# A two-layer block on one Trainium2 core: one projection in every attention slot, and the work between stages and the first x laid out anew

## The reference, cut to what matters

```python
ffn_out = x + gelu(x @ w1 + b1) @ w2 + b2
xq = x + (q_out @ pu_w + pu_b) * abs(q_scale)
out = where(vol > 0.5, xq, ffn_out);  x = layernorm(out) * ln_g + ln_b
```

```python
x = _ln(src) * (1.0 + scale) + shift
scores = q @ k.T / sqrt(32) + attention_bias;  scores = where(src_mask, -inf, scores)
ctx = softmax(scores) @ v
x = x + (ctx @ Wo + bo);  h = _ln(x) * g2 + beta2
return x + _gelu2(h @ W1 + b1) @ W2 + b2
```

## Time and profile before

| | |
|---|---|
| time, median of 3 runs | 2408.28 us (2406.91 to 2420.22) |
| profiled execution | 2410.64 us, its span 2408.8 us, clock granted 0.997 |
| TensorE busy | 98% of the span |
| VectorE, ScalarE, GpSimd busy | 56%, 42%, 42% |
| attention, first slot to the first matmul of L1 | 799.09 to 1685.44 us |

### The profile page before, as it was taken

The page is one execution under the profiler, slowest core; times in us unless marked ns, Lnnn a source line. Parts: engine busy times, 40 slices in busy tenths (PEclk is TensorE's granted clock), DMA queues, the critical chain, the costliest instruction groups (busy, mean ns, idle before and its releaser), DMA issues. The chain is left out here.

```text
span 2408.8 us, 42244 instructions
## 1 busy us (share of the span) xinstructions
PE 2368.5 (98%) x16104; PEld 1896.9 (79%) x16104; DVE 1355.8 (56%) x2749; ACT 1010.2 (42%) x2057; POOL 1018.5 (42%) x829
## 2 busy tenths in 40 slices
PE   9999999999999899999999999998999999999999
PEld 7788888888887677777777777776888888888887
DVE  7354454454457777777777777778443333323332
ACT  6132232231332776767666676767311211111111
POOL 0042241431424896767676776767112112202200
PEclk9999999999999999999999999999999999999999
DMA  7110111101123466565656565574420110110100
GB/s 230 45 44 18 44 35 44 44 17 61 44 80 111 148 192 199 158 209 162 201 163 198 168 200 184 173 209 156 131 71 1 52 52 0 52 52 0 52 35 18
DMA packets 142197, 243.94 MB, mean 101 GB/s; under 512 B 14140, under 2 KB 28620, under 8 KB 142048
## 3 DMA queue, kind: packets, MB, share of 16 engines
q1 hardware_dynamic: 140992, 241.40, 31.3%
q10 hardware_dynamic: 1056, 0.52, 0.1%
HBM read 216.69 MB, written 25.20 MB: 100 GB/s over the span
## 5 line engine op out<-in xcount | busy, mean ns | idle before, releaser
L1251 POOL TENSOR_TENSOR at_bias<-at_bias,at_mask 128x512 f32<-128x512 f32 x512 | 592.7, 1186 | 239.2 <-DMA at_bias<-in_fside_Bx16xSxS 226.7
L647 ACT ACTIVATE L_hid<-bank,L_b1c 128x512 f32<-128x512 f32 x256 | 176.6, 690 | 961.6 <-PE bank L290 961.4
L843 DVE CAST L_hh<-L_hid 128x512 fp32r<-128x512 f32 x256 | 121.7, 475 | 743.2 <-PE bank L970 714.5
L288 PE MATMUL bank<-xth,L_w1h 128*128 128x512 f32 x1024 | 402.7, 393 | 0.5 <-DVE L_w1l L714 0.5
L289 PE MATMUL bank<-xth,L_w1l 128*128 128x512 f32 x1024 | 399.5, 390 | 0.0
L290 PE MATMUL bank<-xtl,L_w1h 128*128 128x512 f32 x1024 | 399.4, 390 | 0.0
L968 PE MATMUL bank<-L_w2h,L_hh 128*128 128x512 f32 x1016 | 398.0, 392 | 0.0
L970 PE MATMUL bank<-L_w2l,L_hh 128*128 128x512 f32 x1016 | 395.6, 389 | 0.0
L969 PE MATMUL bank<-L_w2h,L_hl 128*128 128x512 f32 x1016 | 395.4, 389 | 0.0
L1307 ACT ACTIVATE at_bias<-at_bias,cos_sin 128x512 f32<-128x512 f32 x512 | 363.2, 713 | 3.9 <-DVE cos_sin L1448 3.5
L1448 DVE CUSTOM_DVE_ANT_0 at_bias<-bank,at_bias 128x512 f32<-128x512 f32 x512 | 331.6, 683 | 35.0 <-PE bank L1638 23.5
(11 more groups left out here) (213 smaller groups left out, 3242.2 us busy)
## 6 DMA issues: line engine op xcount, KB each, us to landing
at_bias<-in_fside_Bx16xSxS SPq DMA_DIRECT2D x256, 512.0 KB, 3.6
L_ring<-in_L_cond_w SPq DMA_DIRECT2D x32, 256.0 KB, 5.0
L_xres<-in_x SPq DMA_DIRECT2D x8, 1024.0 KB, 5.3
x_scratch<-L_xres SPq DMA_DIRECT2D x8, 1024.0 KB, 4.3
at_xres<-x_scratch SPq DMA_DIRECT2D x32, 256.0 KB, 4.4
L_xin<-x_scratch SPq DMA_DIRECT2D x8, 1024.0 KB, 5.6
L_xres<-x_scratch SPq DMA_DIRECT2D x8, 1024.0 KB, 5.5
L_xin<-in_x SPq DMA_DIRECT2D x7, 1024.0 KB, 5.1
```

Source lines behind the costliest of these rows:

```text
L288: nc_mm = pe.matmul(out, ah, bh, start=i == 0, stop=False)
L647: nc.scalar.activation(hid[m % 2][:, :], turn[m % 2][:, :], func, bias=b1c[:, m:m + 1]).then_inc(h_act, 1)
L1251: nc.gpsimd.tensor_tensor(tile, tile, mask[:, m % TT, :], ALU.add).then_inc(masked, 1)
```

## The change

Four things are moved; nothing is added to or taken from the arithmetic, except that two of the matmuls on zeros at the start go.

1. The slots of attention. The outputs stand in slots 0, 1, 2 and 3, one each; q and k in 4 to 7, 10, 11, 14 and 15 (batch 0 keeps one more in slot 0, where there is no output yet); v in 8, 9, 12 and 13. Every slot of batches 1 to 6 has exactly one projection. The last four tiles of the next x are turned in slots 5 (two) and 6 (two) instead of 6 (one), 7 (one) and 8 (two). The output of row tile 0 no longer waits for all four `ct_lo` in front of its first step, but for three there and for the fourth in front of step 9.
2. Batch 0 and batch 7. ScalarE's four last norm tiles of L0 go from slots 3 and 4 to 4 and 5, GpSimd's from slots 5 to 8 (one each) to 7 and 8 (two each). ScalarE's four first norm tiles of L1 go from slots 7 and 8 to 7 to 10. The early weights of L1 are shifted by a tile or so.
3. The last batch of L0. The third weight split goes one hidden tile up (ScalarE 13 to 12, VectorE 14 to 13), and so does the mask (13 to 12).
4. The start. SP loads all four column tiles of x, ScalarE's queue loads piece 0 once the identity is there, piece 0 is split in front of column tile 3, and 6 matmuls on zeros stand behind the transposes.

```diff
-    KEYS = {0: (1, 1), 4: (2, 0), 5: (2, 1), 7: (3, 0), 8: (3, 1), 10: (4, 0), 11: (4, 1), 15: (5, 0)}
-    OUTS = {1: (0,), 2: (1,), 3: (2, 3)}
-    VALUES = {9: 0, 12: 1, 13: 2, 14: 3}
-
-    TURNS, LAST_TURNS = {6: (0,), 7: (1,), 8: (2, 3)}, {12: 0, 13: 1, 14: 2, 15: 3}
...
+    KEYS = {4: (2, 0), 5: (2, 1), 6: (3, 0), 7: (3, 1), 10: (4, 0), 11: (4, 1), 14: (5, 0), 15: (5, 1)}
+    FIRST_KEYS = {0: (1, 1), **KEYS}
+    OUTS = {0: 0, 1: 1, 2: 2, 3: 3}
+    VALUES = {8: 0, 9: 1, 12: 2, 13: 3}
+
+    TURNS, LAST_TURNS = {5: (0, 1), 6: (2, 3)}, {12: 0, 13: 1, 14: 2, 15: 3}
...
@@ in output of tensor @@
             if i == 0 and steps[0] == 0:
                 pe.wait_ge(w_lo, 4)
+                pe.wait_ge(ct_lo, b * PHASES + PHASES - 1)
+            if i == 0 and steps[-1] == 3 * KT - 1:
                 pe.wait_ge(ct_lo, b * PHASES + PHASES)
@@ in beside of tensor @@
-                if len(OUTS[m]) == 1:
-                    output(b - 1, OUTS[m][0], some, gen)
-                elif j < 2:
-                    output(b - 1, OUTS[m][0], range(6 * j, 6 * j + 6), gen)
-                elif j == 3:
-                    pe.wait_ge(o_out, b * TT - TT + OUTS[m][1])
-                    output(b - 1, OUTS[m][1], ALL, gen)
+                output(b - 1, OUTS[m], some, gen)
@@ in body of scalar @@
-                if first and m in (3, 4):
-                    for i in (2 * m - 6, 2 * m - 5):
+                if first and m in (4, 5):
+                    for i in (2 * m - 8, 2 * m - 7):
                         f0["last_norm"](1, i)
@@ in beside of vector @@
-            if m in (6, 10, 14):
+            if m in (6, 10, 13):
                 for k in range(KT):
-                    split((m - 6) // 4, k)
+                    split((m - 6) // 3, k)
...
-            if m == 13:
+            if m == 12:
                 for u in range(TT):
                     set_mask(0, u, True)
@@ in start of on_sync @@
             for k in range(KT):
                 cut = slice(k * P, (k + 1) * P)
-                if k % 2 == 0:
-                    sp.dma_start(xin[:, :, cut], rows(x_src[0])[:, :, cut]).then_inc(x0_in[k], 16)
-            for n in range(3):
+                sp.dma_start(xin[:, :, cut], rows(x_src[0])[:, :, cut]).then_inc(x0_in[k], 16)
+            for n in range(1, 3):
                 load_piece(n)
@@ in run of on_scalar @@
-                for k in (1, 3):
-                    cut = slice(k * P, (k + 1) * P)
-                    act.dma_start(xin[:, :, cut], rows(x_src[0])[:, :, cut]).then_inc(x0_in[k], 16)
+                act.wait_ge(setup.ident_in, 16)
+                act.dma_start(piece(0)[3], piece(0)[0]).then_inc(ring_in[0], 16)
                 for k in range(KT):
                     turn_out_of(0, k, first_turn[k])
-                for n in range(TT):
+                    if k == 2:
+                        round_piece(0)
+                for n in range(1, TT):
                     round_piece(n)
```

More of the change, by code:

```diff
@@ L1258, in body @@
                     f0["last_rstd"](1)
-                if first and 5 <= m < 5 + TT:
-                    f0["last_norm"](1, m - 5)
+                if first and m in (7, 8):
+                    for i in (2 * m - 14, 2 * m - 13):
+                        f0["last_norm"](1, i)
                 if last and m == 8:
@@ L1359, in body @@
                         turn_hi(b + 1, 1 - odd, k, turn[0])
-                if before in KEYS:
-                    tile, query = KEYS[before]
+                keys = FIRST_KEYS if first else KEYS
+                if before in keys:
+                    tile, query = keys[before]
                     if tile < KT:
@@ L1366, in body @@
                 if m == 0:
-                    nat_hi_of(b, 1, 0, gen)
+                    nat_hi_of(b, 1, 0 if first else 1, gen)
                 if before in VALUES and not last:
@@ L1513, in body @@
                 if m == 0:
-                    nat_lo_of(b, 1, 0, gen)
+                    nat_lo_of(b, 1, 0 if first else 1, gen)
                 if before in OUTS and not first:
-                    output(b - 1, OUTS[before][-1], gen)
+                    output(b - 1, OUTS[before], gen)
                 if after:
@@ L1530, in body @@
                     turn_lo(b + 1, 1 - odd, LAST_TURNS[m], gen)
-                if m in OUTS and len(OUTS[m]) == 2 and not first:
-                    output(b - 1, OUTS[m][0], gen)
                 if after:
@@ L1691, in beside @@
             some = range(3 * j, 3 * j + 3)
-            if m in KEYS and (KEYS[m][0] < KT or not last):
+            keys = FIRST_KEYS if first else KEYS
+            if m in keys and (keys[m][0] < KT or not last):
                 if j == 0:
                     gen_free(b, m, first)
-                tile, query = KEYS[m]
+                tile, query = keys[m]
                 project(odd if tile < KT else 1 - odd, tile % KT, query, some, gen)
```

40 lines of the change are left out of this document (21 added, 19 removed).

## The result

The changed kernel takes 2398.1 us (median of 7 runs, 2395.1 to 2399.9) where the kernel before takes 2408.2 (7 runs). The ratio is 0.9954 with a 95% interval of 0.9940 to 0.9968: 0.46% faster, 10 us. I had forecast 2394.0 with a range of 2387 to 2402, so the direction and the range hold and the gain is 4 us short of the forecast.

A forecast was written before the change was run, and what follows sets the result against it. TensorE, busy for 98% of the span, was taken as the bound. Terms -8.1 - 3.9 - 0.8 - 1.5 + 0 = -14.3 us on the profiled 2410.64 give 2396.3; that execution was 2.4 above the median, so 2394.0, range 2387 to 2402.

The forecast's parts named there:

- Slots 3 to 8 of batches 1 to 6, -2.05 each: TensorE's attention slots 3 and 5 to 8 fall from 37.65 to 35.60 us a batch, 2.05 less.
- The wait in slot 0, +0.70 each, up to 1.8: In batches 1 to 7 TensorE waits for `ctl` before the output's last third: 0.7 us, at most 1.8.
- my own sign (wrong if it is over 1 us): The prediction called itself wrong if TensorE's new wait for `ctl` in slot 0 was over 1 us.
- a rival for slot 0 alone: GpSimd holds `ctl` in every slot 0: seven waits of 1.8 instead of 0.7, +7.4 us, 2401; chance 0.10.
- Batch 7, -3.9: Batch 7: -2.97 in slot 3, -2.6 in slots 6 to 8, +0.7 in slot 0, +1.0 for the clock.
- 1.0 for the clock: In batch 7, eight slots in a row without a projection may bring back a clock fall: 1.0 of 0 to 1.7 us.
- Batch 0, -0.8 with 1.5 either way: Batch 0: slot gains and losses sum to -0.4, taken as -0.8 us since some of VectorE's lateness goes.
- The third wait: Batch 0, from norms ending slot 5: 0.5 us in slot 6 and 0.4 at its end, 0 to 1.5 in all.
- The end of L0, -1.5: At the end of L0, moving VectorE's split one tile up removes TensorE's wait of 1.47 us: -1.5, no more.
- The start, 0 up to +0.7: At the start, tenths won are given back waiting for `pd`: 0, bounds -0.3 and +0.7 if SP's longer list delays its load.
- The rival that the clock falls after the wait in slot 0: The clock falls after the slot 0 wait in seven batches, 7 x 1.7 = 12 us, 2406; chance 0.07.
- The late x: Next x, wanted at slot 5's end, lands past 13.3 us after its load; each us costs seven, 2421 at 17.2; chance 0.02.

The follow-up runs named there:

- The one-column kernel: Changed kernel with GpSimd's attention mask adds cut to one column, leaving the mask out of the other 511; one run, 2387.8 us.
- the one with slot 8 filled: Changed kernel with twelve matmuls that no one reads put in slot 8 of batch 7; one run, 2397.7 us.
- the early load: Changed kernel with the load of `pd`'s weights issued ahead of the last five weight pieces; one run, 2398.5 us.

## Why the prediction was right, and where it was off

**Slots 3 to 8 of batches 1 to 6, -2.05 each: right.** Slots 5 and 6 are 7.45 and 7.48 (7.50 said), slot 3 7.01, slot 8 6.59. Slot 7 is 7.01 in half of the batches (21 of 42 in seven traces).

**The wait in slot 0, +0.70 each, up to 1.8: right.** It is 0.73 where GpSimd is away, and 0.9 to 1.5 where it isn't. By my own sign (wrong if it is over 1 us), batches 3 and 5 of the profile are just over, with 1.10 and 1.05. Taking for each slot its shortest length over batches 1 to 6, a batch goes from 110.79 to 109.46, -1.33 where I had said -1.35.

**The term that was mis-sized is GpSimd's hold.** I weighed it as a rival for slot 0 alone, in all seven batches or none. It is there in some batches, in slots 0, 7 and 12. The excess over the shortest lengths is 2.1 us in batches 1 to 6 of the kernel before, and 2.0 to 4.1, 3.4 in the mean, in seven traces with the new slots. It costs 1.2 more than before. With it batches 1 to 6 win 6.7 (seven traces, 658.8 to 660.9 against one of before), not 8.1. The one-column kernel, with an excess of 0.1, shows that nothing else is in it. The trace of before could have told me more. I took `ctl` in slot 0 from batch 4 (0.76), while batches 5 and 7 have 0.91 and 1.07; and I named the short waits in slot 12 without asking for their cause. I read the line of `ctl` alone in the earlier trace rows and didn't look at the spread copy, which was held there too:

```profile
L1464 DVE COPY at_normal<-angle x32: 426/700/1519, 820.0 to 1679.4; 128x512 f32<-128x512 f32 x32
```

**Batch 7, -3.9: the sum right, partly by luck.** Batch 7 with L1 won 4.1 in the profile and 4.7 in the mean of six traces (3.4 to 5.9; the one with slot 8 filled left out). But slots 6 to 8 were to lose 2.6, and they lose 0.3 in the profile (22.60 to 22.27) and 0.3 to 1.5 in the six. I had put the empty slot 8 at 6.4; it takes 7.0 to 8.2. With one column of mask it takes 6.50, so what I left out is GpSimd again, and in the profile the clock as well. The other error made up for it. I had added 1.0 for the clock and read only one of its three falls in batch 7 before, which lose 5.1 us together; the six traces lose 0 to 3.4. In the profile slots 12 to 14 are 1.3 shorter and slot 15 with L1 is 0.8 shorter, and I had forecast neither. My sentence that only batch 7 had shown a fall was wrong too, as the trace of before has one at 50 us.

**Batch 0, -0.8 with 1.5 either way: +0.1**, inside its bounds. The wait of 1.45 in front of slot 4 went. But TensorE's wait for the copy of unit 1 in slot 3, which was 1.37 before, is 2.03 now, behind a spread copy of 1.08; in other traces it is 0.5 there with a fall of the clock in slot 2. So slots 3 and 4 together are only 1.3 shorter. The wait in slot 5 is 1.29 where I had 0.78, and the slot is 1.6 longer where I had said 0.9. The third wait, put at 0.9 in and behind slot 6, hardly shows (0.1). Slot 12 is 0.55 longer, which I had not forecast.

**The end of L0, -1.5: the wait of 1.47 went.** Between L270 and the first slot 1.85 was won. I had said that it can't give more than 1.5; where the other 0.35 lies is open.

**The start, 0 up to +0.7: at its upper bound.** L270 starts at 48.8 to 49.6 in eight traces with the new start (mean 49.2), and at 47.8 to 48.4 in four of five with the old one, 49.65 in the fifth (mean 48.5). That is +0.7, uncertain by about 0.3. I had tied this bound to SP's longer list, and the traces fit it: SP issues the load of `pd`'s weights at 12.39 instead of 11.86, and L270 goes with the start of `pd` in 13 traces. That is a connection, not a proof, since the early load gave back only 0.35. What I had said of x is wrong: the first product starts no earlier but at 10.9 to 11.6 in the nine traces with the new start (mean 11.3) and at 10.3 to 11.2 in the five with the old one (mean 10.8). In the nine, TensorE stands for 1.0 to 2.5 us at the transposes (L938) until x lands, in the five for 0 to 0.6.

**The yardstick.** The terms sum to -12.5 in the profiles, 1.8 less than forecast. The other 2.4 of the miss is the step from profile to median: I took the profile of before, 2.4 above its median, and assumed that the changed kernel's would stand so too. It stood on its median. A fall of the clock at 50 us, which half of the traces have, is 1.7 of such a difference.

The rival that the clock falls after the wait in slot 0 didn't come true at 0.7 us, and did in four of seven batches at 2.7 us. The late x didn't come about either, as slots 5 and 6 show no wait.

## What to carry to other kernels

Where one engine is busy for 98% of the span, measure every slot's shortest and usual length apart: the shortest gives the sum, and the difference is contention, which a new order of work changes by itself. Of a VectorE instruction that another engine waits for, or that stands ahead of one, look at whether it works from SBUF to SBUF while GpSimd does too. Here ScalarE did the copy without being held, and six batches won 1.4 us; a place further down VectorE's queue only moved the wait. Compare starts only with the clock's falls taken out, and take more than one trace for anything under 2 us.

## What I had not expected of the hardware

- A single VectorE copy with one SBUF source (128x512, broadcast from 128x16) is held by GpSimd's adds as the one with two sources is: 0.43 us alone, up to 1.57 in the changed kernel and 1.52 before.
- A held copy ends 0.28 to 0.29 us behind the end of a GpSimd instruction, as a rule the one in flight (275 of 384); `ctl` ends 0.55 behind it. Fifteen that started within 0.07 us of that end waited for the next (1.42 to 1.60 us), and one copy missed nine ends in a row, 11.48 us. Why is open.
- GpSimd is held as well: two adds with a copy between them take 2.52 us instead of 2.29.
- ScalarE's copy of the same shape is not held: 616 to 625 ns over 32 of them.
- A stand of TensorE of 2.7 to 2.8 us takes the clock from 1.00 to 0.50 in some batches and not in others, in one execution of one kernel; stands of 0.7 to 1.5 us in slot 0 did so in none of the traces.
